# A step order written out for each engine, one wide drive, and sums moved to TensorE in a decoder layer

## The reference

```
x = layernorm(x + mamba(x));  x = layernorm(x + cross_attention(x, ctx));  x = layernorm(x + moe(x))

mamba: xn = rmsnorm(x); hidden, gate = split(xn @ in_w + in_b)         # 256 inner features each
  conv = silu(4-tap causal convolution of hidden + conv_b)
  ts, B, C = split(conv @ xproj_w)                                     # 64, 16, 16
  delta = softplus(ts @ dt_w + dt_b)
  state[i,n] = exp(A[i,n]*delta[i]) * state[i,n] + delta[i]*B[n]*conv[i]   # over the 64 steps
  y = sum_n state[i,n]*C[n] + D*conv;  out = (y * silu(gate)) @ out_w + out_b
cross_attention: 16 heads of 8 features, 64 queries on 64 keys
moe: softmax router, best 2 of 8 experts, width 176, and one shared expert
```

## Time and profile before

| | |
|---|---|
| three runs | median 2136.62 us (2134.02 to 2137.81) |
| profiled execution | 2137.51 us, span in the trace 2135.7 us |
| granted TensorE clock, mean | 0.928 |
| PE / DVE / ACT / POOL busy | 79% / 81% / 64% / 65% |
| HBM traffic | 65 GB/s over the span |

### The profile page before, as it was taken

How to read it: one execution, slowest core, us unless ns; L and a number is a source line. 1 busy time by engine, 2 the same in 40 slices (tenths; PEclk the granted TensorE clock), 3 DMA queues, 4 the chain that set the end, 5 groups by cost and what they waited for, 6 DMA issues and landing times. The chain is left out here.

```text
span 2135.7 us, 30109 instructions
## 1 busy us (share of the span) xinstructions
PE 1679.3 (79%) x6614; PEld 957.5 (45%) x6690; DVE 1727.6 (81%) x2815; ACT 1363.3 (64%) x4226; POOL 1397.0 (65%) x1300
## 2 busy tenths in 40 slices
PE   2567787978778797888878797887979788787866
PEld 1123454544445454444545444454545445354544
DVE  3789798888888898888988888888989889878523
ACT  3448577584956758485775849567584957647351
POOL 0476676776667677666767766676776767577522
PEclk8769899999999999999999999899999999999988
DMA  3122112222221222222222222212222221222101
GB/s 102 40 64 60 60 62 63 80 66 85 60 75 57 61 80 65 86 60 70 61 62 77 67 85 61 74 57 61 80 64 85 62 77 51 67 73 56 60 6 60
DMA packets 125977, 141.03 MB, mean 66 GB/s; under 512 B 44048, under 2 KB 69456, under 8 KB 125776
## 3 DMA queue, kind: packets, MB, share of 16 engines
q1 hardware_dynamic: 125776, 138.86, 21.8%
HBM read 133.84 MB, written 4.98 MB: 65 GB/s over the span
## 5 line engine op out<-in xcount | busy, mean ns | idle before, releaser
L1078 POOL TENSOR_TENSOR prod<-state,c_rep 128x512 f32<-128x512 f32 x512 | 653.8, 1286 | 192.1 <-DVE state L990 186.0
L990 DVE TENSOR_TENSOR_SCAN state<-decay,p_drive 128x512 f32<-128x512 f32 x512 | 613.9, 1207 | 23.4 <-ACT decay L789 6.5
L591 PE MATMUL p_y<-prod,ident 128*128 128x512 f32 x768 | 433.0, 648 | 71.1 <-POOL prod L1082 45.8
L789 ACT ACTIVATE decay<-delta,a_neg 128x504 f32<-128x504 f32 x512 | 363.8, 720 | 98.3 <-DVE state L990 84.0
L737 ACT ACTIVATE ex<-p_ring,nmax 128x64 f32<-128x64 f32 x1024 | 306.2, 335 | 20.2 <-DVE nmax L915 16.9
L775 ACT ACTIVATE gt<-p_ring 128x512 f32<-128x512 f32 x208 | 124.1, 597 | 216.4 <-PE p_ring L554 216.4
L737 ACT ACTIVATION_READ_ACCUMULATOR ex<-p_ring,nmax 128x1 f32 x1024 | 233.8, 229 | 0.0
L554 PE MATMUL p_ring<-x2T,wg 128*128 128x512 f32 x416 | 225.6, 625 | 7.8 <-DVE km L967 7.7
L554 PE MATMUL p_ring<-x2T,wu 128*128 128x512 f32 x416 | 221.6, 615 | 9.6 <-DVE km L967 8.2
L591 PEld LDWEIGHTS p_y<-prod,ident 128*128 128x128 f32 x768 | 139.1, 204 | 187.0 <-issue 76.3
L1049 POOL TENSOR_TENSOR ex<-ex,rden 128x512 f32<-128x512 f32 x128 | 133.9, 1052 | 122.6 <-DVE rden L919 122.6
(11 more groups left out here) (133 smaller groups left out, 2802.2 us busy)
## 6 DMA issues: line engine op xcount, KB each, us to landing
c_rep<-c_rows SPq DMA_DIRECT2D x256, 256.0 KB, 3.3
cwr<-cw_rows SPq DMA_DIRECT2D x64, 256.0 KB, 3.2
ctxT<-in_ctx_t SPq DMA_DIRECT2D x32, 256.0 KB, 5.0
cwr<-cw_rows SPq DMA_DIRECT2D x32, 224.0 KB, 3.1
cwr<-cw_rows SPq DMA_DIRECT2D x32, 192.0 KB, 2.6
cwr<-cw_rows SPq DMA_DIRECT2D x32, 160.0 KB, 3.0
xf<-in_x SPq DMA_DIRECT2D x16, 256.0 KB, 3.7
xb<-in_x SPq DMA_DIRECT2D x16, 256.0 KB, 4.3
```

What stands on the lines that cost most here:

```text
L591: pe.matmul(p_y[j][:], ident[:], prod[:, k % BUFFERS, :], start=first, stop=n == STATE - 1).then_inc(prod_used.sem, 1)
L789: act.activation(decay[:, j, :].rearrange("p (b t) -> p b t", t=SEQ)[:, :, 1:], delta[:, c.parity, j, :].rearrange("p (b t) -> p b t", t=S ...
L990: dve.tensor_tensor_scan(state[:, k % BUFFERS, :], decay[:, j, :], p_drive[j][:], 0.0, ALU.mult, ALU.add).then_inc(state_ready.sem, 1)
L1078: pool.tensor_tensor(prod[:, k % BUFFERS, :], state[:, k % BUFFERS, :], c_rep[:, n % C_SLOTS, :], ALU.mult).then_inc(prod_ready.sem, 1)
```

## The change

What it does, part by part. (1) `PLAN_TEXT` goes; `ORDER_TEXT` has a list for each engine, in which the pieces of the recurrence are steps like the others. The lists of the engines are cut at different places of the turn. (2) All 20 turns are written out; the loop and its registers go. (3) B's row goes into half 1 of a p_drive of two banks, and one DVE instruction of 128x1024 makes both halves of the drive. The halves are scanned in the order 1, 0. (4) D*h enters p_y as a matmul with a diagonal matrix (`y_d`), so `gated` is one instruction per half. (5) The residuals enter the ring bank as identity matmuls in `mout`, `aout` and `down`; `stats` and `norm` read the bank, and the norm frees it. The down product is two fills of two groups. (6) The first tap is an ACT instruction (`tap`).

```diff
-        p_drive = [bank(f"p_drive{j}") for j in range(HALVES)]
-        p_b = p_drive[0]
+        p_drive = stack.enter_context(nc.psum_tensor("p_drive", [128, HALVES, T], F32))
+        p_b = p_drive[:, 1, :]
...
+            def skip_d(c, i):
+                j = 1 - i
...
+                pe.matmul(p_y[j][:], diag_d[:, j, :], h[:, c.parity, j, :], start=True, stop=False)
...
                 elif name == "mout":
...
                     for g in range(2):
+                        pe.matmul(p[:, g * D:(g + 1) * D], ident[:], xb[:, 2 * i + g, :], start=True, stop=False)
...
+                    for g in range(2):
+                        pe.matmul(p[:, g * D:(g + 1) * D], ident[:], x2[:, 2 * i + g, :], start=True, stop=False)
+                        for j in range(FFN_TILES):
...
+                elif name == "tap":
...
+                    act.activation(zc[:, i, :].rearrange("p (b t) -> p b t", t=SEQ), hpad[:, i, :, 0:SEQ],
+                                   ACT.Identity, scale=w, bias=b).then_inc(tap_first.sem, 1)
...
                 elif name == "km":
                     emptied(act, "k", 0, c.m)
-                    if c.past >= 1:
-                        emptied(act, "down", GROUPS - 1, c.m - 1)
+                    if c.m >= 1:
+                        filled(act, "down", 1, c.m - 1)
...
                 elif name == "norm":
...
+                    p = filled(act, LN_IN[ln], half, c.m)
                     for g in range(2 * half, 2 * half + 2):
-                        a = act.activation(LN_OUT[ln][:, g, :], LN_IN[ln][:, g, :], ACT.Identity,
+                        a = act.activation(LN_OUT[ln][:, g, :], p[:, (g % 2) * D:(g % 2 + 1) * D], ACT.Identity,
                                            scale=rstd[:, ln, g:g + 1], bias=shift[:, ln, g:g + 1])
-                    a.then_inc(ln_ready[ln].sem, 1)
+                    a.then_inc(free(LN_IN[ln], half), 1)
...
+            def drives(c, n):
...
+                dve.tensor_tensor(p_drive[:], u[:, c.parity, :, :],
+                                  p_b.unsqueeze(1).to_broadcast([128, HALVES, T]), ALU.mult
+                                  ).then_inc(drive_ready.sem, 1)
...
-                    dve.scalar_tensor_tensor(yg[:, i, :], h[:, par, i, :], column(V_D + i), p_y[i][:],
-                                             ALU.mult, ALU.add).then_inc(p_y_read.sem, 1)
-                    dve.wait_ge(p_y_read.sem, p_y_read.at(c.m, i))
-                    dve.tensor_tensor(yg[:, i, :], yg[:, i, :], gate[:, par, i, :], ALU.mult
+                    dve.tensor_tensor(yg[:, j, :], p_y[j][:], gate[:, par, j, :], ALU.mult
                                       ).then_inc(yg_ready.sem, 1)
-                elif name == "down":
-                    p = filled(dve, name, i, c.m)
-                    dve.tensor_tensor(x2[:, i, :], p[:, 0:D], x2[:, i, :], ALU.add).then_inc(free(name, i), 1)
```

More of the change, by code:

```diff
@@ L191, in ring_place @@
     same = [j for j in range(bank, len(RING), BANKS)]
-    if not isinstance(m, int):
-        per_turn = len(same)
-        ahead = sum(CHUNK_OF[RING[j][0]] - CHUNK_OF[stage] for j in same)
-        return bank, m * per_turn + (ahead + sum(j < at for j in same))
     t = m - CHUNK_OF[stage]
@@ L356, in build @@
         gt_ready, act_ready = signal("gt_ready", FFN_TILES), signal("act_ready", ROUTED)
-        LN_IN, LN_OUT = (xb, x1b, x2), (x1, x2, x2)
+        LN_IN, LN_OUT = ("mout", "aout", "down"), (x1, x2, x2)
         def column(at):
@@ L451, in step @@
                                      ).then_inc(cw_in[i % CW_SLOTS].sem, 16)
-            def turn(chunks):
-                for s in range(STEPS):
-                    for stage, name, i in PLAN[s]:
-                        if stage in chunks:
-                            step(name, i, chunks[stage])
-            turns(sp, turn)
+            turns("sp", step)
             sp.wait_ge(out_done.sem, out_done.at(CHUNKS - 1))
@@ L594, in turn @@
-            def turn(chunks):
-                for s in range(STEPS):
-                    if s % 2 == 1:
-                        n = (s + 1) // 2 % STATE
-                        if ("scan" if n else "front") in chunks:
-                            spread_b(chunks["scan" if n else "front"], n)
-                    own = [e for e in PLAN[s] if e[0] in chunks]
-                    for e in own[:1]:
-                        step(e[1], e[2], chunks[e[0]])
-                    k = (s - SUM_LAG) % STEPS
-                    if ("scan" if s >= SUM_LAG else "back") in chunks:
-                        sum_n(chunks["scan" if s >= SUM_LAG else "back"], k)
-                    for e in own[1:]:
-                        step(e[1], e[2], chunks[e[0]])
@@ L612, in _ @@
+                mm.then_inc(ring_full[r].sem, 1)
+            turns("pe", step)
         @block.scalar
@@ L617, in _, with decays @@
             act.wait_ge(consts_v.sem, CONSTS)
+            def decays(c, k):
+                n, first = divmod(k, HALVES)
+                j = 1 - first
+                if k == 0:
+                    act.wait_ge(delta_ready.sem, delta_ready.at(c.m))
+                if n > 0 or c.m >= 1:
+                    act.wait_ge(state_ready.sem, state_ready.at(c.m, k - HALVES))
+                act.activation(decay[:, j, :].rearrange("p (b t) -> p b t", t=SEQ)[:, :, 1:],
+                               delta[:, c.parity, j, :].rearrange("p (b t) -> p b t", t=SEQ)[:, :, 1:],
+                               ACT.Exp, scale=a_neg[:, j, n:n + 1]).then_inc(decay_ready.sem, 1)
             def step(name, i, c):
```

379 lines of the change are left out of this document (153 added, 226 removed), and 62 rows, old and new, of the table ORDER_TEXT.

## The result

Four runs of the changed kernel have a median of **2050.47 us** (2047.89 to 2052.62), beside 2137.22 (2134.02 to 2138.50) for four of the kernel before. The ratio is 0.9600, with a 95% interval of 0.9579 to 0.9621. The forecast was 1972, the range 1930 to 2058: the sign is right, the gain is 87 us where 165 were forecast, and the time lies near the range's slow end, some 11 us from rival 1 (2061). The profiled execution took 2052.2, its span is 2050.4.

What follows compares the result with a forecast made beforehand. No single engine bound the kernel: PE led A, ACT B, DVE C. 124.2 + 1.6 - 11.9 - 3.6 = 110.3 us, plus 2.7 friction: 113.0; 274 + 15 x 113.0 = 1969, stated as 1972 us, range 1930 to 2058.

Steps and rivals of the forecast that it cites:

- rival 1: Attention stays loose: score products stand behind sums waiting for POOL; turn 119 us, time 2061 us; chance 0.19.
- A: Window from `gated` to first score maximum, 24.0 us before, on PE: first exp at 26.4 instead of 24.8, +1.6 us.
- B: Attention window until the router's first instruction, 60.9 us before, on ACT: -11.9 us, called an order's gain.
- the walk: Stretch-by-stretch sum of one turn on its leading engines, every hand-over in B just in time: 110.3 us.
- C: Window of router and up products, 39.3 us before, on DVE: 35.3 to 35.8 us, -3.6 us.
- friction: Allowance for imperfect hand-overs in B: 2.7 us a turn, a third of ACT's 7.8 us idle before.
- DVE busy 1590: DVE's busy time over the whole changed kernel, forecast near 1590 us.
- Wide drive: One DVE instruction of 128x1024 at 1.25 us for two narrow ones, saving 0.2 us 16 times a turn: 3.2 us.
- Filling and draining: Time outside the 15 turns: 281.2 us before, about 5 less filling and 2 less draining, 274 us.
- Rival 3: Straight-line code starves an engine, one gap of 2.76 us per turn: turn 115.8, time 2013 us; chance 0.05.
- Rival 4: Banks of `down`, held through the norm, keep PE from q or v: slower, 2141 us at 14 us delay; chance 0.05.
- Rivals 2 and 5: No friction at all, turn 110.3 or below, 1930 us, chance 0.10; no effect, within 0.2%, chance 0.02.

Runs made afterwards that it cites:

- e1: The kernel before with all 20 turns written out, nothing else: 2125.19 us, ratio 0.9940 to the kernel before.
- e2: The changed kernel's new order, written out, with the old operations on DVE again (not word for word): 2106.59 us, ratio 0.9858 to the kernel before.
- e5: The changed kernel with DVE's second score maximum ahead of silus and gate, and ACT's gate copy behind the second exp: 2043.72 us.
- e11: The changed kernel with e5's edit, the D*h products moved late into PE's gap, and two idle products behind them: 2005.98 us.
- e12: e11 without the sum (r_sum + 1e-20) ahead of the router's second reciprocal: 1993.31 us, ratio 0.9342 to the kernel before.
- e4: The changed kernel plus, behind its last output, five kinds of DVE instruction six times each, with POOL idle and then busy: 2114.47 us.
- e8: The changed kernel with two drive instructions of 128x512 again, without the old semaphore wait between them: 2052.29 us.
- e9: The changed kernel with the residual sums on DVE again, two groups in one instruction: 2055.03 us.
- e7: The changed kernel with three idle 128x512 products on PE ahead of the second turned copy of x2: 2028.79 us.

## Why the prediction was right, and where it missed

The sign is right, and so is the shape of A and B: A longer, B shorter, though by half of what the walk had. C is shorter only beside a C with a jump in it; beside that of e1 (36.6) it is longer, where the forecast had it 1 us shorter than 36.5. Taken by the forecast's own cuts in the turn shown, it missed 6.4 us a turn:

| | forecast | measured | |
|---|---|---|---|
| first exp behind `gated` | 26.4 | 27.2 | +0.8 |
| router's maximum behind it, with 2.7 of friction | 51.0 | 54.0 | +3.0 |
| C | 35.5 | 38.2 | +2.7 |

The medians over turns 2 to 14 are 27.2, 55.0 and 37.9. The prediction named B above 55 us by waits of PE for POOL as a sign of being wrong: by the cut of the earlier trace rows the median B is 55.8, with such waits, so this sign came. That the time still lies in the range is owed to the range reaching as far as rival 1.

- **A.** The walk's times hold: km starts on ACT 18.0 us behind `gated` (forecast 17.4), the first exp 9.1 later (9.0). In part this is luck: the walk followed ACT's list from km on, and the exp waits for a score product that waits 1.31 us for POOL's masks, which the walk did not price. "Here DVE's saving is worth nothing" is wrong. The walk took for granted that DVE keeps up; e2 shows that in the new order it does not without the new operations, and this is where they earn most.
- **B is "an order's gain".** Right as to cause, by e2: the order alone takes B from 60.9 to 56.2, and the operations bring 0.4 more. Wrong in size. The view by windows of the changed kernel, ACT alone, from the first exp to the end of the softplus and from there to the router's maximum (length, ACT busy, granted clock, DMA):

```profile
1121.15:1171.10 49.95, 45.78 (x184) 0.99 0.27 75
1171.10:1175.14 4.04, 3.17 (x6) 0.50 0.00 0
```

  ACT's work was forecast at 45.3 and is 45.8; what the walk lacked is 4.2 of idle time, 1.9 of it for the held gate. Behind it norm, copy and router product took 4.0 instead of 3.0, at half clock (0.50). The friction of 2.7 was the mis-sized term: 5.7 was wanted in this turn, 6.7 in the median. That it is not one wait that can be taken away is shown by e5.
- **C.** The term "35.3 to 35.8" was DVE's work at its unheld prices and with PE at full clock. The changed kernel has neither: r_sel, r_max and r_cw are held for some 2.1 us (684, 965 and 1050 ns against 192, 170 and 195), and DVE waits 2.03 us for a product at half clock. With PE busy in the gap e11's C is 36.8, and with one held instruction left out as well e12's is 35.5; that this is the forecast's figure is chance, as it is reached with one instruction less and two others still held.
- **DVE busy 1590** missed by 97: the means of the held groups (silus, gates, other taps, shifts and the router's three) grew by some 115 us in sum. The price of 1.1 for a multiplication from SBUF in the earlier trace rows was itself a held one: alone it is 0.69 (e4).
- **Wide drive**: 1.22 measured for 1.25, and the Trainium skill's "VectorE: DVE Perf Modes", The TRN2 errata, gives an estimate of 1.19. The saving of 0.2 was right too (1.42 to 1.22 from start to end), but two thirds of it are the semaphore wait between the halves and not the width, and e8 shows no time gained by the width.
- **Filling and draining** came to 261 and not 274.
- **Rivals.** Rival 1's turn of 119 was met (119.3), its mechanism only in part. It had 57.0 from the first exp to the router's maximum, where 54.0 came; A and C, which it left as they were, brought the rest. B is loose by waits of PE for POOL's scaled exps and for the norms, and by a low clock at its end, but not by the sums waiting for POOL, as rival 1 said: that idle time fell from 71.1 to 6.0 us. PE's waits in the changed kernel (total, times, longest):

```profile
PE p_ring L575 <- POOL ex L1056: 73.7, 32, 3.5
PE p_ring L551 <- ACT x L791: 62.2, 17, 4.0
```

  Rival 3 falls by e1. Rival 4, the ring held through the norm, did not come: the kernel is faster, and A is 26.4 as walked. e9 frees the banks early and is not faster, but it also gives DVE six sums back, so it does not price the hold alone. Rivals 2 and 5 did not come.

## What to carry to other kernels

Before an instruction is moved or an order changed, see which DVE instructions have two operands in SBUF and what POOL runs beside them; a short one on the engine that leads can cost six times its own time. Where TensorE idles some microseconds ahead of a chain that others wait for and its granted clock falls, try giving it work, even useless work, and better a product that needs no fixed place; then look at the clock in every turn, since one turn can show the cure and the next not. A saving that one undo shows as worthless may still be worth something together with others: ask how much slack it fits into, and whether the undo puts back the waits too.

## What the runs showed of the hardware

- A DVE product of 128x512 with both operands in SBUF takes 0.69 us alone, the same as with one in PSUM, and 1.63 beside POOL's products; a 128x2 one 0.16 and, in the kernel, up to 1.22 in the rows above. POOL pays as well: two products beside the silus took 3.38 us, where two take 2.5 otherwise.
- A `tensor_scalar` of 128x4, with a single operand, is held (170 to 660 ns); a reciprocal of 128x8 is not (203 and 203).
- 48 products whose results nobody reads made the kernel 1% faster (2050 to 2029 us), by TensorE's clock at the end of B and the start of C. Three of them a turn kept the clock at 2.4 GHz there in 6 of 15 turns (e7); the two D*h products and two such ones did in all 15 (e11).
- Two independent DVE products of 128x512 start 0.60 us apart, with 0.69 each; with a semaphore wait between them, 0.73 apart.
